# Attention scored twice on one core: score maxima kept as one 16-bit value, reduced a whole row at a time, and three single score banks

## What is computed

```python
attn = jnp.einsum('bqd,bkd->bqk', q, k) / np.sqrt(HD)      # 48 (image, head) pairs, 1024 x 1024
attn = (attn.reshape(b * NH, h, w, h, w) + rel_bias_h[:, :, :, :, None] + rel_bias_w[:, :, :, None, :]).reshape(b * NH, hw, hw)
attn = jax.nn.softmax(attn, axis=-1)
out = jnp.einsum('bqk,bkd->bqd', attn, v)
```

## Time and profile before

| what | us |
|---|---|
| median of 3 runs | 901.74 (898.37 to 903.61) |
| the profiled execution | 902.66 |
| its span on the core, first to last instruction | 900.8 |
| PE busy | 795.0 (88%) |
| DVE busy | 744.4 (83%) |
| ACT busy | 559.2 (62%) |
| POOL busy | 423.6 (47%) |
| reductions of pieces, L1073, 768 of them | 483.0 |
| exponents, L1036, 384 of them | 372.0 |

### The profile page before, as it was taken

The page is one execution under the profiler, slowest core; times in us unless marked ns, Lnnn a source line. Parts: engine busy times, 40 slices in busy tenths (PEclk is TensorE's granted clock), DMA queues, the critical chain, the costliest instruction groups (busy, mean ns, idle before and its releaser), DMA issues. The chain is left out here.

```text
span 900.8 us, 15301 instructions
## 1 busy us (share of the span) xinstructions
PE 795.0 (88%) x5848; PEld 411.9 (46%) x5848; DVE 744.4 (83%) x1493; ACT 559.2 (62%) x609; POOL 423.6 (47%) x263
## 2 busy tenths in 40 slices
PE   4899475679999999999999999999999999678874
PEld 2655365234444444444444444444444442356643
DVE  6998846698899999888899989999898894079995
ACT  1333336036777777777777777777777778347773
POOL 3677795435373544537363736445463323012220
PEclk9999668699999999999999999999999999789986
DMA  7676599999559392939477684939294000333411
GB/s 193 208 218 204 172 289 392 267 180 199 107 110 190 74 198 65 197 72 207 94 165 137 131 170 92 186 79 202 56 209 81 13 12 16 130 106 123 140 36 53
DMA packets 65739, 130.06 MB, mean 144 GB/s; under 512 B 9529, under 2 KB 45370, under 8 KB 57210
## 3 DMA queue, kind: packets, MB, share of 16 engines
q1 hardware_dynamic: 57634, 115.95, 56.6%
q10 hardware_dynamic: 8032, 13.13, 4.1%
HBM read 89.73 MB, written 34.60 MB: 138 GB/s over the span
## 5 line engine op out<-in xcount | busy, mean ns | idle before, releaser
L1073 DVE TENSOR_REDUCE at_piece_neg<-at_r_ps 128x1 f32<-128x512 f32 x768 | 483.0, 682 | 60.8 <-PE at_r_ps L943 57.6
L1036 ACT ACTIVATE at_probs<-at_s_ps 128x1024 f32<-128x1024 f32 x384 | 372.0, 1021 | 132.8 <-PE at_s_ps L964 131.5
L943 PE MATMUL at_r_ps<-op_mix_k,op_mix_q 128*128 128x256 f16 (+1 forms) x1920 | 281.9, 257 | 23.1 <-DVE at_piece_neg L1073 10.3
L857 POOL COPY op_mix_q<-op_mix_q 2x4096 f16<-2x4096 f16 x48 | 172.7, 3599 | 233.9 <-ACT op_mix_q L1041 233.3
L943 PEld LDWEIGHTS at_r_ps<-op_mix_k,op_mix_q 128*128 128x128 f16 x1920 | 148.3, 98 | 288.3 <-DVE at_piece_neg L1073 194.1
L964 PE MATMUL at_s_ps<-op_mix_q,op_mix_k 128*128 128x512 f16 x768 | 227.6, 379 | 1.1 <-ACT at_probs L1036 0.5
L978 PE MATMUL at_o_ps<-at_probs,op_v_u 128*32 128x512 f32 x1536 | 204.1, 604 | 0.0
L219 POOL MEMSET op_mix_q<- 2x10240 f32 x12 | 103.5, 8628 | 0.6
L964 PEld LDWEIGHTS at_s_ps<-op_mix_q,op_mix_k 128*128 128x128 f16 x768 | 73.5, 98 | 19.4 <-ACT at_probs L1036 10.7
L1041 ACT ACTIVATE op_mix_q<-at_r_ps 2x1024 f16<-2x1024 f16 x48 | 48.6, 1012 | 51.9 <-PE at_r_ps L954 51.9
L861 POOL TENSOR_TENSOR at_o_sb<-at_o_sb,at_inv_rows 128x512 f32<-128x512 f32 x24 | 30.6, 1276 | 86.1 <-DVE at_inv_rows L1100 86.1
(11 more groups left out here) (121 smaller groups left out, 680.4 us busy)
## 6 DMA issues: line engine op xcount, KB each, us to landing
op_mix_q<-qk_parts SPq DMA_DIRECT2D x48, 640.0 KB, 10.8
op_mix_q<-bias_parts SPq DMA_DIRECT2D x120, 120.0 KB, 10.2
op_mix_q<-bias_parts SPq DMA_DIRECT2D x72, 128.0 KB, 10.2
qk_parts<-op_mix_q SPq DMA_DIRECT2D x24, 256.0 KB, 2.4
v_rows<-pr_v_st SPq DMA_DIRECT2D x8, 768.0 KB, 4.1
op_mix_k<-qk_parts SPq DMA_DIRECT2D x48, 128.0 KB, 13.2
op_v_u<-v_rows SPq DMA_DIRECT2D x12, 512.0 KB, 14.5
op_mix_q<-bias_parts SPq DMA_DIRECT2D x24, 256.0 KB, 11.0
```

The lines of the kernel that those rows point to most:

```text
L857: pool.tensor_copy(rows[:, 1:, :, :], rows[:, 0:1, :, :].to_broadcast([2, ops.VARIANTS - 1, 2, GROUP])).then_inc(max_spread, 1)
L943: last = pe.matmul(r_bank("piece", at)[:, first % GROUP:first % GROUP + n], mix_q[owner.buf][:, variant, j, qt * P:(qt + 1) * P], mix_k[ow ...
L1036: act.activation(probs[n % PRING][:, 2 * pair:2 * pair + 2, :], s_ps[pair][:, :, :], ACT.Exp).then_inc(exp_done, 1)
L1073: dve.tensor_reduce(piece_neg[half][:, i:i + 1], r_bank("piece", at)[:, :], AX_X, ALU.max, negate=True).then_inc(reduced, 1)
```

## The change

- **One 16-bit value.** The maximum is kept as one rounded 16-bit value, which the exponent pass subtracts. DVE writes it straight from the reduction: `join_max` and its three operations go. The two rows at `MAX_ROW` now hold two heads of a pair, and `mix_k` has a pattern of ones and zeros (`parity`) there in place of ones, so that each head takes its own row. Making it costs POOL one more operation on 2x1024 elements in the bias phase in place of an identity and a pick matrix that nothing used, and SyncE 8 copies in place of 5 (`load_hot`).
- **Whole rows.** `score_row` makes a whole query row of 1024 keys with the same five matmuls, into one of two pairs of banks (`RRING` = 2); `reduce_row` reduces all 1024 at once. A unit has 32 rows, two in every step.
- **Turned once a half.** `turn` stands at steps 6 and 14, and its 8 transposes carry all four heads. It uses a score bank.
- **Three single score banks** (`SRING` = 3). Scores of one head take one bank, and ACT takes 768 exponents of 128x512. Turns and scores share one numbered ring (`use_of`).
- **Order.** On PE a step is now scores, row, scores, scores, row, scores, weigh. On POOL `spread_max` is three copies, for variant 0 (the odd heads), variants 1 and 2, and variants 3 and 4, and `zero_max` stands ahead of `normalise` of the unit before. On SyncE that unit's store stands between `load_qkv` and `load_bias`.

```diff
     PRING = 4
-    PIECES = QUAD * KT * 2
...
+    ROWS = QUAD * 2 * TILES
+    PER_STEP = ROWS // STEPS
...
-    RING = 3
+    SRING, RRING = 3, 2
...
-        piece_neg = [ph.sb(f"piece_neg{h}", [P, PIECES // 2], F32) for h in range(2)]
-        row_neg = [ph.sb(f"row_neg{h}", [P, QUAD * TILES], F32) for h in range(2)]
...
+        neg_max = [ph.sb(f"neg_max{h}", [P, QUAD // 2, TILES, 2], F16) for h in range(2)]
...
-        s_ps = [ph.ps(f"s_ps{i}", [P, 2, GROUP], F32) for i in range(2)]
-        r_ps = [ph.ps(f"r_ps{i}", [P, GROUP], F32) for i in range(RING)]
+        s_ps = [ph.ps(f"s_ps{i}", [P, GROUP], F32) for i in range(SRING)]
+        r_ps = [ph.ps(f"r_ps{i}", [P, 2, GROUP], F32) for i in range(RRING)]
...
-        def pieces(n):
-            at = PIECES // 2 + (LEAD + n) * PER_STEP
+        def rows_of(n):
+            at = ROWS // 2 + (LEAD + n) * PER_STEP
             return list(range(at, at + PER_STEP))
...
+        TURN_AT = ((2 * KT - LEAD + 1) % STEPS, KT - LEAD + 1)
+        ROWS_BEFORE = (0, 1, 1, 2, 2)
...
-        BEFORE, AFTER = (0, 1, 1, 2, 2), 3
...
+        use_of = {("turn", 0): 0}
...
+        for u in range(UNITS):
...
+                for half in (1, 0):
+                    if n == TURN_AT[half] and (half == 1 or u + 1 < UNITS):
+                        use_of["turn", u * 2 + 1 if half else (u + 1) * 2] = len(use_of)
+                for j in range(QUAD):
+                    use_of["scores", u * STEPS + n, j] = len(use_of)
+        def turn_use(unit, half):
+            return use_of["turn", unit.u * 2 + half]
+        def max_rows(use):
+            return s_ps[use % SRING][:, :].bitcast(F16)[0:2, :].rearrange("p (g t) -> p g t", g=QUAD // 2)
...
+        SPREADS = ((0, 1), (1, 3), (3, 5))
...
-            def spread_max(unit, half, pair):
...
-                pool.tensor_copy(rows[:, 1:, :, :], rows[:, 0:1, :, :].to_broadcast([2, ops.VARIANTS - 1, 2, GROUP])).then_inc(max_spread, 1)
+            def spread_max(unit, half):
+                rows = mix_q[unit.buf][MAX_ROW:MAX_ROW + 2, :, :, half * GROUP:(half + 1) * GROUP]
+                pool.wait_ge(s_taken, turn_use(unit, half) + 1)
+                pool.tensor_copy(rows[:, 0, 1::2, :], rows[:, 0, 0::2, :]).then_inc(max_spread, 1)
+                pool.wait_ge(max_spread, spreads_done(unit, half, 0))
+                for first, last in SPREADS[1:]:
+                    pool.tensor_copy(rows[:, first:last, :, :], rows[:, 0:1, :, :].to_broadcast([2, last - first, QUAD, GROUP])).then_inc(max_spread, 1)
...
                 if unit.u + 2 < UNITS:
                     need(pool, pv_done, unit.u * STEPS)
                     ops.zero_max(pool, unit.after(2).buf)
-                spread_max(unit, 1, 1)
+                if not unit.first:
+                    pool.wait_ge(max_spread, spreads_done(unit, 0, ops.VARIANTS - 1))
+                    pool.wait_ge(ops.max_zeroed, min(unit.u + 3, UNITS))
+                    normalise(unit.after(-1), 1)
+                    pool.wait_ge(norm_done, unit.u * 2)
+                spread_max(unit, 1)
+                pool.wait_ge(max_spread, spreads_done(unit, 1, ops.VARIANTS - 1))
+                normalise(unit, 0)
+                pool.wait_ge(norm_done, unit.u * 2 + 1)
                 if not unit.last:
-                    spread_max(unit.after(1), 0, 0)
...
-                    spread_max(unit.after(1), 0, 1)
+                    spread_max(unit.after(1), 0)
...
+                nxt = unit.after(2)
                 if unit.first:
                     for stored in ops.bias_stored:
                         sp.wait_ge(stored, 32 * 2)
...
+                if nxt.u < UNITS:
                     need(sp, pv_done, unit.u * STEPS)
-                    load(unit.after(2))
+                    ops.load_qkv(sp, nxt.image, nxt.buf)
+                if not unit.first:
+                    store(unit.after(-1), 1)
+                if nxt.u < UNITS:
+                    ops.load_bias(sp, nxt.u, nxt.buf)
                 store(unit, 0)
...
+            def score_row(unit, at):
+                owner, i = (unit, at) if at < ROWS else (unit.after(1), at - ROWS)
+                j, qt = i // TILES % QUAD, i // (ROWS // 2) * TILES + i % TILES
+                count = unit.u * ROWS + at
+                need(pe, reduced, count - RRING + 1)
                 for variant, first, n in ops.SEGMENTS:
+                    last = pe.matmul(r_ps[count % RRING][:, first // GROUP, first % GROUP:first % GROUP + n],
+                                     mix_q[owner.buf][:, variant, j, qt * P:(qt + 1) * P],
+                                     mix_k[owner.buf][:, j, first:first + n], start=True, stop=True)
+                last.then_inc(row_scored, 1)
+            def turn(unit, half):
+                use = turn_use(unit, half)
+                pe.wait_ge(reduced, unit.u * ROWS + (half + 1) * (ROWS // 2))
+                need(pe, s_taken, use - SRING + 1)
+                for pair in range(QUAD // 2):
+                    for t in range(TILES):
+                        last = pe.transpose(max_rows(use)[:, pair, t * P:(t + 1) * P], neg_max[half][:, pair, t, :], ident16[:, :])
+                last.then_inc(s_filled, 1)
...
             def scores(unit, n, j):
                 half, kt = n // KT, TILE_ORDER[n % KT]
...
+                use = use_of["scores", unit.u * STEPS + n, j]
+                need(pe, s_taken, use - SRING + 1)
                 keys, queries = slice(kt * P, (kt + 1) * P), slice(half * GROUP, (half + 1) * GROUP)
...
+                pe.matmul(s_ps[use % SRING][:, :], mix_k[unit.buf][:, j, keys], mix_q[unit.buf][:, ops.VARIANT_OF[kt], j, queries],
+                          start=True, stop=True).then_inc(s_filled, 1)
...
-                    if n % KT == 2:
-                        pe.wait_ge(max_spread, unit.u * 4 + (n // KT + 1) * 2)
...
+                    variant = ops.VARIANT_OF[TILE_ORDER[n % KT]]
+                    if variant in (0, SPREADS[1][0], SPREADS[2][0]):
+                        pe.wait_ge(max_spread, spreads_done(unit, n // KT, variant))
...
+                    if n == TURN_AT[1]:
+                        turn(unit, 1)
+                    if n == TURN_AT[0] and not unit.last:
+                        turn(nxt, 0)
                     for j in range(QUAD):
...
                         scores(unit, n, j)
...
+                        for at in todo[ROWS_BEFORE[j]:ROWS_BEFORE[j + 1]]:
+                            score_row(unit, at)
...
-                for pair in range(2):
-                    act.wait_ge(scores_done, step * 2 + pair + 1)
-                    act.activation(probs[n % PRING][:, 2 * pair:2 * pair + 2, :], s_ps[pair][:, :, :], ACT.Exp).then_inc(exp_done, 1)
...
+                for j in range(QUAD):
+                    use = use_of["scores", step, j]
+                    act.wait_ge(s_filled, use + 1)
+                    act.activation(probs[n % PRING][:, j, :], s_ps[use % SRING][:, :], ACT.Exp).then_inc(s_taken, 1)
+            def row_max_in(unit, half):
+                use = turn_use(unit, half)
+                act.wait_ge(s_filled, use + 1)
+                act.activation(mix_q[unit.buf][MAX_ROW:MAX_ROW + 2, 0, 0::2, half * GROUP:(half + 1) * GROUP],
+                               max_rows(use), ACT.Copy).then_inc(s_taken, 1)
...
-                dve.tensor_reduce(piece_neg[half][:, i:i + 1], r_bank("piece", at)[:, :], AX_X, ALU.max, negate=True).then_inc(reduced, 1)
...
+            def reduce_row(unit, at):
+                owner, i = (unit, at) if at < ROWS else (unit.after(1), at - ROWS)
+                half, r = divmod(i, ROWS // 2)
+                j, t = divmod(r, TILES)
+                count = unit.u * ROWS + at
+                need(dve, row_scored, count + 1)
+                if r == 0 and owner.u > 0:
+                    dve.wait_ge(s_filled, turn_use(owner.after(-1), half) + 1)
+                dve.tensor_reduce(neg_max[half][:, j // 2, t, j % 2:j % 2 + 1], r_ps[count % RRING][:, :, :].rearrange("p h t -> p (h t)"),
+                                  AX_X, ALU.max, negate=True).then_inc(reduced, 1)
...
```

216 lines of the change are left out of this document (48 added, 168 removed).

## The result

The changed kernel takes 878.84 us (median, 876.27 to 882.17), against 901.0 us for the kernel before beside it: a ratio of 0.9741, 95% interval 0.9717 to 0.9765. It is faster by 22 us, where 15.5 were forecast. The ratios compare fast executions alone: two disturbed ones of `e_turn_mid` and one of the kernel before are left out. Its profiled execution took 880.72 us, with a span of 878.9, against 902.66 and 900.8. The span is 21.9 us shorter, and where that came from is read from marks on PE, each the start of the same weigh in both traces, and from the end.

The account below looks back on a forecast made before the run. PE was taken as the bound, busy 48.46 of 49 us a unit. Old turns 28.6 plus DVE waits 11.6, less new turns 20.7 and the end's 4.0, gave 15.5 us off 902.66: 887 as median, range 879 to 899.

Parts of the forecast that it names:

- Plain step: PE's step without a turn: the same matmuls in another order, still 2.84 us.
- ACT: Exponents of 512 in single banks: 0.60 us long, 0.49 apart; score 3 has 0.40 us to spare, no cost.
- POOL: The three spread_max copies and the clearing end before they are needed; cover thinnest for the first copy.
- SyncE: Bias loads begin about 10 us later, needed some 30 us on: covered.
- Turns: Two a unit in place of four, each costing 0.94 us against 0.65, with PE waiting 0.30 for ACT's copy.
- The rival in which ACT's copy is hidden: A turn costs 0.65 us, 6.4 us more gained: 881; chance 0.10.
- DVE: Whole-row reductions and no joins remove three PE waits, 1.05 us a unit; the needed reduction ends 0.15 us early.
- The rival that priced a row at 1.22: A row costs DVE two of the old reductions, 6.6 us less gained: 894; chance 0.12.
- Start: Up to step 5 of unit 0: nothing gained, PE's wait for unit 1's loads growing to 5 us or more.
- End: From step 5 of unit 11, without rows: steps of 2.45 us, score 3 waiting for exponent 0; 4.0 us lost.
- The clock: Rival: PE's clock falls to 1.2 GHz at the end, 17 us lost: 904, no change; chance 0.05.
- Last phase: Behind attention's last weigh: the forecast's sum had no term for it.

Follow-up runs that it names:

- e_turn_mid: Changed kernel with the turn moved from ahead of score 0 to between scores 1 and 2 of the same step; 0.9739 of the kernel before.
- e_late_start: Changed kernel with the first three reductions ahead of unit 0 done twice; 0.9751 of the kernel before.
- e_turn_order: Changed kernel with turn steps reordered: both rows one place forward, weigh ahead of score 3; 874.14 us, 0.9686 of the kernel before.
- e_tail_ring: Changed kernel with the four row banks joining the score and turn ring from step 5 of the last unit; 0.973 of the kernel before.
- e_two_reductions: Changed kernel with each row reduced by two reductions of 512, only the second's maximum going on, no join; 0.9757 of the kernel before.

## Why the prediction was right or wrong

The direction was right and the place too; the gain was 21.9 us of span, where the sum had 15.5, and the median is 878.84 us, where the forecast was 887 and its lowest 879. By its steps:

- **Plain step, ACT, POOL, SyncE:** right. 2.84; exponents 0.60 long and 2.17 for four; score 3 never waits in the middle; no wait for POOL's copies.
- **Turns: the step that failed.** The forecast said that a turn would cost 0.94, and it costs 0.73. The wait for ACT's copy is 0.31, as forecast (0.30). Mis-sized is the place of the transposes: the forecast put them 0.10 behind the end of the weigh, where a score would start. Their weights of two columns are loaded under the weigh (515.86), and they start 0.88 us after its start (516.28), where a score starts 0.99 to 1.00 after it (513.56 behind 512.56). That is 0.21 earlier, and everything behind moves with it. 22 x 0.21 = 4.6 us, and the sum becomes 24.1, against 23.78 measured. The rival in which ACT's copy is hidden came close in its number, 881, by luck: the wait is there.
- **DVE: right outcome, wrong reason.** All three waits are gone, and the reductions are 1.218 long and 1.14 apart (2.36 for two). But the runs show that a row at two reductions, even with the joins, leaves at most 0.1 us a unit, and that one bank fewer brings the waits back. What the forecast called the cause, and its margin of 0.15 us, decided nothing, and that the waits went as forecast was luck; the row ring went from three banks to four. The rival that priced a row at 1.22 and lost 6.6 us by it was wrong for the same reason: two reductions of 512 cost 539.42 - 538.26 = 1.2 us between step 6 of unit 0 and the last weigh. The Trainium skill's figure, "VectorE: DVE Perf Modes", section on the TRN2 errata, gave an estimate of 1.19 for a reduction of 1024: the trace lies on both sides of it, 1.218 alone and 1.14 in a row, and nothing hung on it.
- **Start:** right, 0.27 gained. The wait for the loads is 3.90 and not the 5 or more that I named, and PE ran the step behind it at half speed: from 207.0 to 209.9 the granted clock is 0.50, and the step is 1.4 us longer than in `e_late_start`. The forecast had no term for that.
- **End:** right, 3.81 lost for 4.0. The clock did not fall: it is 1.00 while PE works 24.89 of 29 us.
- **Last phase:** forecast at nothing, 1.66 us gained. Its granted clock differs from run to run (0.86 to 0.88 between 762 and 874 us in the changed kernel, `e_turn_mid`, `e_turn_order`, `e_tail_ring`, `e_two_reductions` and `e_late_start`), and why it was better here is open.

On the turn's place: 0.10 is what the gap is in the kernel before, where the turn stands behind a piece. There the transposes start 0.32 after the piece does (506.72), while a score starts 0.22 after one (510.77 to 510.99):

```profile
506.40 0.39 PE L943 MATMUL at_r_ps<-op_mix_k,op_mix_q 128*128 128x256 f16 x2
...
510.99 0.59 PE L964 MATMUL at_s_ps<-op_mix_q,op_mix_k 128*128 128x512 f16 x2
```

Behind the weigh that gap is not there. The kernel with the turn's order changed says the same without a wait for ACT: its turn costs 0.43, which is 0.54 less 0.11.

The missing 6.4 us are 4.3 in the middle, 0.3 at the start, 0.2 at the end, 1.7 behind attention.

## What to carry to other kernels

When the engine in the middle waits for a consumer's work that comes in lumps, count banks before you count instructions: a fourth row bank absorbed DVE's lumps of 0.6 and 0.9 us in neighbouring steps. With it the consumer's own saving was worth 0.1 us a unit; the joins cost 5.5 us with three banks in the new order and nothing with four. An operation that blocks a ring slot for a microsecond is cheapest where the most independent work lies between it and the slot's next user; moving one weigh and two rows was worth 0.3 us a turn without touching any operation. Where a stretch runs out of filler work, let its ring take over the banks that the filler leaves.
